# A fused attention, recurrence and expert block: VectorE's side work moved one step down beside the second alignment

## What is computed

```
x = x + _L0_xattn_ref(ctx_1024, _layernorm(x, axis=-1))
x = x + _L0_attn_ref(_layernorm(x, axis=-1), Wr, Wk, Wv, Ww, Wo)
x = x + _L0_ffn_ref(_layernorm(x, axis=-1), gate_w, w1, w2, w3, sw1, sw2, sw3)
```

```
cd, cu, cl = R[i - 1, j - 1], R[i - 1, j], R[i, j - 1]
choice = jnp.argmin(jnp.stack([cd, cu, cl]))
...
contrib = small[i_idx] * valid[:, None]
expanded = jnp.zeros((T_large, d)).at[j_idx].add(contrib)
```

## Time and profile before

| | us |
|---|---|
| median of 3 runs | 1249.31 |
| lowest, highest | 1246.77, 1251.16 |
| the profiled execution | 1247.96 |
| its span | 1246.7 |
| TensorE busy | 1019.6 (82%) |
| VectorE busy | 703.9 (56%) |
| ScalarE busy | 484.2 (39%) |

### The profile page before, as it was taken

How to read it: one execution, slowest core, us unless ns; L and a number is a source line. 1 busy time by engine, 2 the same in 40 slices (tenths; PEclk the granted TensorE clock), 3 DMA queues, 4 the chain that set the end, 5 groups by cost and what they waited for, 6 DMA issues and landing times.

```text
span 1246.7 us, 15709 instructions
## 1 busy us (share of the span) xinstructions
PE 1019.6 (82%) x4832; PEld 619.7 (50%) x4832; DVE 703.9 (56%) x2431; ACT 484.2 (39%) x854; POOL 83.4 (7%) x113
## 2 busy tenths in 40 slices
PE   5886639888550899977988579886999999999998
PEld 2332213333210555543755355654677777777776
DVE  4985659999899665695669412437322222222226
ACT  4884617767660445323321245232222222222221
POOL 1000000000000000000000000000122222222210
PEclk9998969999785899889889689798999999999999
DMA  9999955447787788330000297493011100111114
GB/s 366 305 288 302 220 129 156 145 137 179 225 214 191 244 277 300 107 122 1 1 17 1 89 330 256 140 361 124 22 35 34 35 30 31 34 35 35 30 38 182
DMA packets 119328, 179.77 MB, mean 144 GB/s; under 512 B 7984, under 2 KB 91408, under 8 KB 119184
## 3 DMA queue, kind: packets, MB, share of 16 engines
q1 hardware_dynamic: 115504, 168.54, 44.2%
q0 software_dynamic: 3744, 10.23, 2.5%
HBM read 154.32 MB, written 24.42 MB: 143 GB/s over the span
## 4 chain that ended last, share of the span: by engine, by line
PE 38%; DVE 8%; DMA 2%; issue 1%; ACT 1%; DVEq 0%; ACTq 0%
PE bank L1632 17%; PE bank L1658 10%; PE bank L1490 3%; PE bank L1643 3%; DMA rows_c<-ctx_nat_dram 2%; PE bank L1511 2%; DVE beyond L722 2%; DVE passed L727 1%; PE bank L1601 1%; DVE beyond L721 1%; PE bank L1587 0%; PE bank L1748 0%; PE bank L1569 0%; DVE hid L908 0%; DVE hidT L915 0%
## 5 line engine op out<-in xcount | busy, mean ns | idle before, releaser
L1632 PE MATMUL bank<-w_up,srcT 128*128 x624 | 197.4, 459 | 0.6 <-ACT srcT L1282 0.6
L908 DVE TENSOR_TENSOR hid<-bank,act_s 128x352 f32<-128x352 f32 x110 | 57.4, 524 | 213.8 <-PE bank L1632 208.8
L1632 PEld LDWEIGHTS bank<-w_up,srcT 128*128 128x128 f32 x624 | 117.8, 189 | 54.9 <-issue 0.8
L1419 PE MATMUL bank<-sq,ones 128*64 128x402 f32 (+1 forms) x512 | 105.7, 536 | 41.3 <-ACT sq L1149 41.3
L1290 ACT ACTIVATE act_s<-bank 128x352 f32<-128x352 f32 x110 | 50.7, 463 | 226.0 <-PE bank L1632 225.9
L1435 PE MATMUL bank<-table,ident 128*128 128x402 f32 x144 | 68.5, 559 | 74.5 <-DVE stays L676 67.8
L1413 PE MATMUL bank<-ctxT,latT 128*64 128x402 f32 (+1 forms) x512 | 104.1, 529 | 22.1 <-DMA ctxT<-ctx_tr_dram 21.4
L1658 PE MATMUL bank<-w_dn,hidT 128*128 (+1 forms) x468 | 114.0, 380 | 0.4 <-DVE y_sb L929 0.4
L1490 PE MATMUL bank<-rows_c,on_path 128*64 128x256 f32 (+1 forms) x832 | 103.5, 402 | 10.5 <-DMA rows_c<-ctx_nat_dram 9.6
L1149 ACT ACTIVATE sq<-ctxT 128x1608 f32<-128x1608 f32 x64 | 97.5, 1526 | 16.9 <-DMA ctxT<-ctx_tr_dram 16.9
L1182 ACT ACTIVATE code<-bank,unpassed 128x402 bf16<-128x402 f32 x72 | 42.3, 592 | 138.7 <-PE bank L1437 138.7
(11 more groups left out here) (255 smaller groups left out, 1452.6 us busy)
## 6 DMA issues: line engine op xcount, KB each, us to landing
rows_c<-ctx_nat_dram SPq DMA_DIRECT2D x32, 896.0 KB
ctxT<-ctx_tr_dram SPq DMA_DIRECT2D x32, 804.0 KB, 8.0
ctxT<-ctx_tr_dram SPq DMA_DIRECT2D x32, 797.0 KB, 8.5
rows_c<-ctx_nat_dram SPq DMA_DIRECT2D x32, 640.0 KB
spaced<-dist SPq DMA_DIRECT2D x128, 101.0 KB, 5.7
w_up<-w_t_dram SPq DMA_DIRECT2D x16, 704.0 KB, 12.2
table<-spaced SPq DMA_DIRECT2D x16, 404.0 KB, 11.2
w_dn<-w_t_dram SPq DMA_DIRECT2D x16, 256.0 KB, 4.4
```

Source lines behind the costliest of these rows:

```text
L908: e.tensor_tensor(hid[i][:, :], psum[2 * i + 1][:, 0:HH], act_s[i][:, :], ALU.mult).then_inc(hid_done, 1)
L1419: last = e.matmul(ps[b * T:(b + 1) * T, 0:nq], ones[:, 0:T], sq[i][:, b, k, 0:nq], start=False, stop=(k == KC - 1))
L1632: last = e.matmul(psum[2 * i + m][:, 0:HH], lhsT, rhs, start=(k == 0), stop=(k == KC - 1))
```

## The change

One step without an instruction is put into VectorE's list of side work, behind `add_rows(0..3)` and ahead of the first recurrence. The lists of ScalarE, TensorE and SyncE stay as they were.

```diff
+def pause():
+
+    yield
 ...
-            interleave(align(1), chain(add_rows(range(0, 4)), together(recurrence(0), add_rows(range(4, 8))),
+            interleave(align(1), chain(add_rows(range(0, 4)), pause(), together(recurrence(0), add_rows(range(4, 8))),
                                        beside(recurrence(1), experts(RUNS[0]), shared_beside), experts(RUNS[1])),
                        behind_second)
```

## The result

| | before | changed |
|---|---|---|
| median | 1248.67 us (20 runs) | 1242.49 us (20 runs) |
| lowest, highest | 1239.00, 1253.05 | 1237.08, 1252.81 |
| the profiled execution | 1247.96 | 1241.54 |
| its span | 1246.7 | 1240.3 |

The ratio changed to before is 0.996, 95% interval 0.9943 to 0.9977: some 5 us faster, where 1.9 were forecast.

The account below looks back on a forecast made before the run. VectorE's list of work plus its waits was taken to bound the stage up to 699 us. Gains of 0, 1.6 and 0.3 sum to 1.9 us, giving a forecast median of 1247.4 us, range 1243.4 to 1250.9.

Parts of the forecast that it names:

- First recurrence: 466 to 543 us: VectorE's added lead is lost at the `col_min` buffers; gain 0 to 0.4 us, taken as 0.
- The 0.8 by which the third `kv` write should lag: End of the forward pass: `hn` and the projections come 0.8 us later, so the wait for `kv` ends at 572.65.
- the ring: Two `col_min` buffers limiting VectorE's lead in the first recurrence; the wait near 531 us grows to 1.6 to 2.3.
- End of the forward pass: 543 to 581 us: last comparison `stays` moves ahead of scan and product, last `code` write at about 579.5; gain 1.6 us.
- the second half takes 1.7: TensorE's last block comparison, end of the forward pass: its second half takes 1.7 us, from 1.5 between starts before.
- Second recurrence: 581 to 639 us: VectorE's added backward slots fit into its waits; gain 0.3 us, 1.9 in all at 639.
- the two slots in hand: Second recurrence: VectorE has done two more backward alignment steps when the experts begin, 1.9 us, kept behind the long `hid` wait.
- TensorE has no pause up to 635 that VectorE could end: Experts, from about 605 us: VectorE does not hold TensorE, so both extra slots stay in hand behind the `hid` wait.
- 639 to 699: `hidT` lands 1.8 us later, TensorE about 2 later within its 9.96 of slack; `path_terms` is ready 1.9 earlier.
- Rival A: Longer pause at 639 us slows two first-stage groups, each costing about 1, together the 1.9: 1249.3 us; chance 0.15.
- B: Shorter pause before 698.99 lets the first tile run at 3.24 instead of 5.45: 1245.2, or 1242.2 us; chance 0.23.
- C: From 702 us on, two more groups of 28 matmuls fall to the lower clock: 4.1 slower, 1253.4 us; chance 0.07.

Follow-up runs that it names:

- g1: The kernel before, run again unchanged: median 1248.05 us, ratio 1.0013 to before.
- g2: The changed kernel, run again unchanged: median 1240.47 us, ratio 0.9962 to before.
- g3: The kernel before, plus 4 matmuls whose result nobody reads in TensorE's pause ahead of the last comparison: 1242.84 us, ratio 0.9961.
- f3: The kernel before, with only side steps 10 and 11 of the second recurrence one slot later: 1242.45 us, ratio 0.9956.
- f2: The kernel before, with the empty step put ahead of the second recurrence only: 1240.80 us, ratio 0.9947.
- g4: The kernel with the empty step ahead of the second recurrence only, plus 7 idle matmuls ahead of the wait for `path_terms`: 1241.46 us, ratio 0.9957.
- h2: The kernel before, plus 4 idle matmuls ahead of the last comparison and 7 ahead of the second sums of squares: 1239.06 us, ratio 0.9944.
- f1: The changed kernel without the first recurrence's last empty step, so VectorE's order is that of before from the second recurrence on: 1247.20 us, ratio 1.000.
- h1: The changed kernel, plus 7 idle matmuls on TensorE ahead of the second sums of squares: 1238.15 us, ratio 0.9925.
- m2: The changed kernel with 7 idle matmuls ahead of the second sums of squares, run a second time: 1239.77 us, ratio 0.9929.
- f4: The changed kernel, plus 9 idle matmuls on TensorE behind the wait for `path_terms`: 1249.85 us, ratio 1.0022.

## Why the prediction was right and where it was wrong

The sign and the places were right, the size was not: 1.9 forecast, 5.0 measured; the median of 1242.49 lies 0.9 under the lower end of the range (the median of before, with more runs, itself lies 0.6 under the 1249.31 that the range started from; 0.996 of 1249.31 is 1244.3, inside it). Within 0.3% had the largest chance; the ratio is just beyond it.

**First recurrence: 0, right.** 74.20 and 74.21 from the first to the third `kv` write. The `col_min` wait grew to 1.69 at 529.18 (1.6 to 2.3 forecast), TensorE's wait for `hn` from 0.95 to 1.96. That this `hn` would come later in absolute time (0.7) is seen only between g1 and g2: from the first `kv` write to `lg` 43.03 and 43.63 us. In the first two profiles it came 1.7 earlier, because in the kernel before half of the `w_o` products there took 3.78 us and 1.99 in the changed. The 0.8 by which the third `kv` write should lag did not show: 74.12 and 74.22 in g1 and g2. In the changed kernel VectorE is held by the ring at two more places, 1.06 at 514.64 and 1.33 at 547.40, which the prediction had not foreseen. VectorE did lag, and more than forecast: the last `hn` ahead of the third `kv` write starts 60.52 us behind the first `kv` write in g1 and 62.93 in g2. But in g1 TensorE was still at the slow comparison behind its wait of 5.11 and took `hn` up at 63.51, in g2 at 63.70. In the first two profiles that `hn` starts at 62.85 and 62.92, for `lg` had come later in the kernel before (45.37 against 43.98, the slow products). So matmuls at the lower level in the kernel before covered the lag, different ones in each execution; that the two stretches are equal is in part luck.

**End of the forward pass: 1.6 forecast, 3.0 measured.** The forecast had `kv` 0.8 later and the last `code` write 6.85 behind it (572.65, 579.5). Measured are no lag and 6.22. So 1.4 us were missing: 0.8 is the lag, and 0.6 is a duration. The earlier trace rows have the half comparison of 128x201 at 0.88, almost the 0.96 of one twice as wide. I took the 1.5 between the starts at 578.70 and 580.21 as what the second half costs, although that is a half-rate duration, and forecast it again ("the second half takes 1.7") behind a pause that the change removes. In the changed profile it takes 0.87, from 576.49 to 577.36. The step that failed here is this one: the durations of matmuls behind a removed pause were carried over unchanged. What moved the `stays` forward was right, but at equal clock it is worth 1.40 only; 1.62 of the 3.02 came because the clock no longer fell there (g3), and the sum named the clock at two other places only.

**Second recurrence: 0.3 forecast, 2.0 measured.** The mechanism was right link by link, except that VectorE did hold TensorE once before 635; the first link's error passed through it. Changed less before, measured from the third `kv` write (which both reach 74.2 us after the first); the forecast has its lag of 0.8 in it:

| place | forecast | measured |
|---|---|---|
| fourth `kv` write | -1.4 | -3.08 |
| `rms`, behind one more slot | -0.2 | -1.94 |
| last `xr` of the recurrence, first `hid` | -0.2 | -2.56 |
| the `hid` with the long wait | -0.2 | -3.13 |
| `path_terms`, behind two slots less | -1.9 to -2.1 | -5.04 |

The added slot cost 1.14, the two slots in hand gave 1.91 (1.9 forecast). TensorE's lead at the fourth `kv` write is 1.7 larger than forecast, 1.4 of it from the step above. Of the rest, 0.6 is clock: the 16 products of `w_o` took 5.87 us instead of 6.48. And 0.6 was held by VectorE, against "TensorE has no pause up to 635 that VectorE could end". TensorE's groups of an expert, the kernel before and then the changed:

```profile
606.64 2.53 PE L1632 MATMUL bank<-ws_up,h2T 128*128 128x352 f32 x8
610.89 2.53 PE L1632 MATMUL bank<-ws_up,h2T 128*128 128x352 f32 x8
...
618.88 2.53 PE L1632 MATMUL bank<-ws_up,h2T 128*128 128x352 f32 x8
623.23 2.53 PE L1632 MATMUL bank<-ws_up,h2T 128*128 128x352 f32 x8
```

```profile
604.21 2.53 PE L1637 MATMUL bank<-ws_up,h2T 128*128 128x352 f32 x8
608.21 2.53 PE L1637 MATMUL bank<-ws_up,h2T 128*128 128x352 f32 x8
...
616.20 2.53 PE L1637 MATMUL bank<-ws_up,h2T 128*128 128x352 f32 x8
620.19 2.53 PE L1637 MATMUL bank<-ws_up,h2T 128*128 128x352 f32 x8
```

In the changed kernel the steps are 4.00 apart; before, two of them are 4.25 and 4.35, the second with a wait of 0.17 for `hidT`. Every profile with the order of before has this (29.98 to 30.26 us from the first `hid` to the one with the long wait), every one with the changed order and a slow last group does not (29.41 to 29.66). In sum: 1.9 as forecast, 0.8 for the lag that did not come, 0.6 for the half comparison and 0.6 for the products at a higher rate, 0.6 for this hold, 0.5 not put down to anything.

f3, where only the first part of the shift is made, has -3.08 at the fourth `kv` write and -3.03 at `path_terms`: it pays no slot and gains none.

**639 to 699, right.** `hid` waits 6.54, TensorE waits 6.29 for `hidT` (about 6 forecast), no wait for `hid` appears behind it that costs the path. VectorE's waits from 466 to 699 sum to 5.1 us less (55.8 before, 50.7 changed), where 2 were forecast. The wait for `path_terms` fell to 7.57 instead of 6 to 7, and ended 3 earlier than the 697 of the forecast. Rival A fell with that: the slow group of 16 behind the longer pause took 5.30 us, less than the 6.24 before; in f2 it took 6.67, and still no wait for `hid` followed.

**The rivals of the clock.** B had the sign and the number (1242.2), at the wrong place. It put the clock's gain behind `path_terms`, where g4 shows none, and the sum left out the pauses ahead of it. C's mechanism exists (a group of 28 at 731.38 took 6.22 before; all later ones 3.24 in the changed profile, but 4.93 at 740.11 in g2) but where it strikes changes from one execution to the next. The Trainium skill, "TensorE: Matmul & The Clock Gate", section "Why this matters for your kernels", asks that pauses between bursts of matmuls be kept short. The prediction used this for the two long pauses alone. g3 and h2 agree with it for the pause of 2.94 (filled: 0.84; left: 1.54 in the kernel before), f1 does not (left, and 0.84 all the same).

## What to carry to other kernels

Before a sum takes over a matmul's duration, compare it with equal or wider ones in the same profile: if it is half rate behind a pause, and the change removes the pause, the duration changes too, and with it everything that waits for that engine. Where a pause of TensorE stands ahead of short work on the path, and its length is set by another engine, idle matmuls in it are a cheap trial; they belong ahead of the wait that ends the pause, and are to be fewer than fill it. When whole runs scatter by more than the effect, measure the distance between two events of the stage that was changed: here it repeated within 0.25 us for the kernels before and changed (and within 1.9 for h1 and m2), where times scattered by 14. Such a distance says nothing of what lies outside it: f1's D is 2.1 shorter than before, its time is not.

## What the runs showed of the hardware

- Adding work made the kernel faster: four matmuls that compute nothing, 0.39% (g3); eleven, 0.56% (h2).
- The same pause of 2.94 us ahead of the same comparison was followed by the lower level of the clock in two executions (9.24 and 8.78 to the last `code` write) and by the upper in a third (f1, 7.62). A pause makes the fall possible, not certain. Of the groups of 28 matmuls fed by `rows_c`, one behind a pause of 1.76 took 4.93 us (g2, 740.11), one behind 2.79 in the same profile 3.24 (721.93).
- Where the clock falls moves from execution to execution of one program: the products of `w_o` took 6.51 us in h1 and 3.96 in m2.
- After a pause of 7.56 us, 18 entries of uninterrupted matmuls took 0.52 us each and not 0.35, and the group after them still was slower than full rate (f4).
- Shortening a pause need not keep the clock up: with the granted clock at 1.00 in the idle matmuls ahead of it, a pause of 2.84 us was followed by 0.50 (g4).
